# Cross-attention on one core: matmul operands of 1, 4 and 52 rows filled up to 128, and a 103-column transpose

## The reference

```python
text_p  = einsum('bld,dh->blh', H_l, W_text) + b_text      # x: 4 x 2048 x 512
audio_p = einsum('bsd,dh->bsh', H_a, W_audio) + b_audio    # ctx: 4 x 77 x 384
Q = layer_norm(text_p, g1, beta1)
K = layer_norm(audio_p, g2, beta2)
V = audio_p
scores  = einsum('blh,bsh->bls', Q, K) / sqrt(512)
alpha   = softmax(scores)
H_hyper = einsum('bls,bsh->blh', alpha, V)
H_hyper = einsum('blh,hk->blk', H_hyper, W_out) + b_out
return layer_norm(H_hyper + H_l, g_out, beta_out)
```

## Time and profile before

| | us |
|---|---|
| median of 3 runs | 270.38 |
| lowest and highest run | 270.07, 270.52 |
| the profiled execution's span | 269.2 |
| PE busy | 253.6 (94%) |
| DVE busy | 234.1 (87%) |
| ACT busy | 207.2 (77%) |
| POOL busy | 207.4 (77%) |

### The profile page before, as it was taken

The page is one execution under the profiler, slowest core; times in us unless marked ns, Lnnn a source line. Parts: engine busy times, 40 slices in busy tenths (PEclk is TensorE's granted clock), DMA queues, the critical chain, the costliest instruction groups (busy, mean ns, idle before and its releaser), DMA issues.

```text
span 269.2 us, 5946 instructions
## 1 busy us (share of the span) xinstructions
PE 253.6 (94%) x1667; PEld 232.3 (86%) x1667; DVE 234.1 (87%) x719; ACT 207.2 (77%) x516; POOL 207.4 (77%) x232
## 2 busy tenths in 40 slices
PE   7799999999999999999999999999999999999750
PEld 6578878989999989999999999999999999999520
DVE  3867489978999998999999999999999999998594
ACT  3766348235788888989988898888889889999681
POOL 6057440011189999999999999999999999999985
PEclk9999999999999999999999999999999999999997
DMA  6926099532225553544555445444444455442217
GB/s 195 266 80 195 2 280 393 151 131 72 78 80 168 167 175 138 175 160 157 177 181 179 168 169 173 165 156 156 156 158 159 169 169 162 160 171 108 106 46 273
DMA packets 19456, 43.25 MB, mean 161 GB/s; under 512 B 2050, under 2 KB 2382, under 8 KB 19434
## 3 DMA queue, kind: packets, MB, share of 16 engines
q1 hardware_dynamic: 18810, 41.96, 46.6%
q10 hardware_dynamic: 624, 1.06, 1.4%
HBM read 21.19 MB, written 16.78 MB: 141 GB/s over the span
## 4 chain that ended last, share of the span: by engine, by line
PE 73%; POOL 11%; DVE 5%; DMA 5%; ACT 2%; issue 2%; SPq 1%; POOLq 0%; ACTq 0%; DVEq 0%
PE psY L1332 24%; PE psY L1343 11%; PE psT L1261 9%; PE psO L1355 9%; PE psY L1336 4%; DMA zs<-in_ctx_dram 3%; POOL zs L464 3%; POOL zs L458 3%; PE psE L1311 2%; PE psE L1312 2%; DMA xs<-in_x_dram 2%; PE psY L1153 2%; POOL rstd L470 2%; POOL zs L494 1%; POOL zs L498 1%
## 5 line engine op out<-in xcount | busy, mean ns | idle before, releaser
L1332 PE MATMUL psY<-proj,x_hi 128*128 128x336 f32 x512 | 103.1, 323 | 0.0
L1332 PEld LDWEIGHTS psY<-proj,x_hi 128*128 128x128 f32 x512 | 82.7, 189 | 5.6 <-issue 0.4
L464 POOL TENSOR_TENSOR zs<-zs,shift 128x512 f32<-128x512 f32 x54 | 68.6, 1292 | 0.0
L458 POOL TENSOR_TENSOR zs<-zs,gain 128x512 f32<-128x512 f32 x54 | 68.5, 1290 | 0.0
L470 POOL TENSOR_TENSOR rstd<-stat_eps,neg_half 128x4 f32<-128x4 f32 x30 | 30.5, 1017 | 37.8 <-DVE stat_eps L970 35.9
L1343 PE MATMUL psY<-proj,x_lo 128*128 128x336 f32 (+1 forms) x256 | 50.7, 320 | 0.0
L958 DVE CUSTOM_DVE_ANT_0 waste_dve<-psY,xs,sums 128x515 bf16<-128x515 f32 x64 | 48.4, 756 | 2.3
L662 ACT ACTIVATE zs<-hid,shift,rstd 128x512 f32<-128x512 f32 x59 | 47.9, 812 | 0.0
L978 DVE SCALAR_TENSOR_TENSOR hid<-psO,inv_sum,xs 128x512 f32<-128x512 f32 x60 | 44.8, 746 | 2.0 <-PE psO L1355 0.8
L620 ACT ACTIVATE x_hi<-psT 128x512 fp32r<-128x512 f32 x64 | 38.1, 595 | 9.0 <-PE psT L1261 6.9
L856 DVE TENSOR_TENSOR x_lo<-psT,x_hi 128x512 fp32r<-128x512 f32 x64 | 43.6, 681 | 0.6 <-ACT x_hi L620 0.6
(11 more groups left out here) (264 smaller groups left out, 420.2 us busy)
## 6 DMA issues: line engine op xcount, KB each, us to landing
xs<-in_x_dram SPq DMA_DIRECT2D x64, 256.0 KB, 2.9
out_dram<-zs SPq DMA_DIRECT2D x29, 512.0 KB, 2.9
proj<-proj SPq DMA_DIRECT2D x4, 768.0 KB, 9.4
out_dram<-zs SPq DMA_DIRECT2D x6, 256.0 KB, 2.1
xs<-in_L_xattn_W_text_dram SPq DMA_DIRECT2D x4, 256.0 KB, 4.2
xs<-in_L_xattn_W_out_dram SPq DMA_DIRECT2D x2, 512.0 KB, 4.2
wa<-in_L_xattn_W_audio_dram SPq DMA_DIRECT2D x1, 768.0 KB, 6.7
zs<-in_ctx_dram SPq DMA_DIRECT2D x1, 462.0 KB
```

The source lines that it names most:

```text
L458: nc.gpsimd.tensor_tensor(zs[:, q, t, :], zs[:, q, t, :], gain[:], ALU.mult).then_inc(zg_ready, 1)
L464: nc.gpsimd.tensor_tensor(zs[:, q, t, :], zs[:, q, t, :], shift[:], ALU.add).then_inc(out_ready, 1)
L1332: nc.tensor.matmul(psY[:, t, to:to + HALF], x_hi[:, par, t, k * P:(k + 1) * P], proj[:, q, k, right * HALF:(right + 1) * HALF], start=(k = ...
```

## The change

Operands with fewer than 128 rows get 128. The tiles `cd_rows`, `pick` and `root_rows` have 128 partitions, and POOL fills them with zeros ahead of the writes to rows 0 to 3 or row 0. `kSqSum` gets 76 more columns, filled with zeros, so that line 1246 reads 128 columns in each block. The diagonals get all 128 rows in the last block as well (`krstd` has 128 rows already). A semaphore `zeros_ready` is raised four times by POOL and waited for by ACT, DVE and PE. The second transpose of `transpose_prob` and of the last step takes 103 columns in place of 128. `keep_busy` writes to another quarter of its bank.

```diff
-        cd_rows = sb("cd_rows", [4, 2, BS], F32R)
-        pick = sb("pick", [4, 2, P], F32R)
+        cd_rows = sb("cd_rows", [P, 2, BS], F32R)
+        pick = sb("pick", [P, 2, P], F32R)
...
-        kSqSum = borrow(0, BS)
+        kSqSum = borrow(0, len(KEYS) * P)
+        kSqLive, kSqPad = kSqSum[:, 0:BS], kSqSum[:, BS:len(KEYS) * P]
...
-        root_rows = x_hi[0:1, 0]
+        root_rows = x_hi[:, 0]
...
             nc.gpsimd.memset(mask[:], 1.0).then_inc(pool_own, 1)
+            nc.gpsimd.memset(kSqPad, 0.0).then_inc(zeros_ready, 1)
...
+            nc.gpsimd.memset(f32(root_rows), 0.0).then_inc(zeros_ready, 1)
+            nc.gpsimd.memset(f32(pick[:]), 0.0).then_inc(zeros_ready, 1)
+            nc.gpsimd.memset(f32(cd_rows[:]), 0.0).then_inc(zeros_ready, 1)
             pool.wait_ge(left_ready, 2)
...
+            act.wait_ge(zeros_ready, 4)
+            nc.scalar.activation(root_rows[0:1, 1, :], ROOT_BANK[0:1, :], ACT.Copy, scale=-1.0).then_inc(root_rows_ready, 1)
+            nc.scalar.activation(root_rows[0:1, 0, :], ROOT_BANK[0:1, :], ACT.Copy).then_inc(root_rows_ready, 1)
...
-                nc.vector.tensor_scalar(diag_hi[0:w, at:at + w], ident[0:w, 0:w], krstd[0:w, n:n + 1], None, ALU.mult).then_inc(diag_ready, 1)
+                nc.vector.tensor_scalar(diag_hi[:, at:at + w], ident[:, 0:w], krstd[:, n:n + 1], None, ALU.mult).then_inc(diag_ready, 1)
...
+            dve.wait_ge(zeros_ready, 4)
             for n in range(2):
-                nc.vector.tensor_tensor(pick[:, n, :], ident[0:4, n:n + 1].to_broadcast([4, P]),
+                nc.vector.tensor_tensor(pick[0:4, n, :], ident[0:4, n:n + 1].to_broadcast([4, P]),
...
-                    nc.tensor.matmul(bank[:, 0:P], ident[:], ident[:], start=True, stop=True)
+                    nc.tensor.matmul(bank[:, 3 * P:4 * P], ident[:], ident[:], start=True, stop=True)
...
-                        last = nc.tensor.matmul(A_BANK[0][:, at:at + w], ones_r[0:w, :], d[0:w, at:at + w], start=(n == 0), stop=(n == 1))
+                        last = nc.tensor.matmul(A_BANK[0][:, at:at + w], ones_r, d[:, at:at + w], start=(n == 0), stop=(n == 1))
...
+            pe.wait_ge(zeros_ready, 1)
             for n, (at, w) in enumerate(KEYS):
-                last = nc.tensor.matmul(A_BANK[1][0:w, n:n + 1], kSqSum[:, at:at + w], mean_of[:, 0:1], start=True, stop=True)
+                last = nc.tensor.matmul(A_BANK[1][:, n:n + 1], kSqSum[:, at:at + P], mean_of[:, 0:1], start=True, stop=True)
...
-                    last = nc.tensor.transpose(psE[:, (2 * t + 1) * P:(2 * t + 2) * P], f32(parts[:, t, 0:P]), ident[:])
+                    last = nc.tensor.transpose(psE[0:S + S_B, (2 * t + 1) * P:(2 * t + 2) * P], f32(parts[:, t, 0:S + S_B]), ident[:])
```

More of the change, by code:

```diff
@@ L193, in cross_attention @@
         ident_ready, ones_ready, gain_ready = sem("ident_ready"), sem("ones_ready"), sem("gain_ready")
+        zeros_ready = sem("zeros_ready")
         cxT_psum, cxT_ready = sem("cxT_psum"), sem("cxT_ready")
@@ L576, in _ @@
             act.wait_ge(root_psum, 1)
-            nc.scalar.activation(root_rows[:, 1, :], ROOT_BANK[0:1, :], ACT.Copy, scale=-1.0).then_inc(root_rows_ready, 1)
-            nc.scalar.activation(root_rows[:, 0, :], ROOT_BANK[0:1, :], ACT.Copy).then_inc(root_rows_ready, 1)
+            act.wait_ge(zeros_ready, 4)
+            nc.scalar.activation(root_rows[0:1, 1, :], ROOT_BANK[0:1, :], ACT.Copy, scale=-1.0).then_inc(root_rows_ready, 1)
+            nc.scalar.activation(root_rows[0:1, 0, :], ROOT_BANK[0:1, :], ACT.Copy).then_inc(root_rows_ready, 1)
             out_hi(1)
@@ L642, in _ @@
             act.wait_ge(cd_rows_psum, 1)
-            nc.scalar.activation(cd_rows[:, 0, :], C_BANK[0:4, 0:BS], ACT.Copy).then_inc(cd_hi_ready, 1)
+            nc.scalar.activation(cd_rows[0:4, 0, :], C_BANK[0:4, 0:BS], ACT.Copy).then_inc(cd_hi_ready, 1)
             score_hi(3)
@@ L865, in _ @@
                     dve.wait_ge(ksqsum_ready, k - 1)
-                nc.vector.tensor_tensor(kSqSum, kSq0 if k == 1 else kSqSum, KSQ[k], ALU.add).then_inc(ksqsum_ready, 1)
+                nc.vector.tensor_tensor(kSqLive, kSq0 if k == 1 else kSqLive, KSQ[k], ALU.add).then_inc(ksqsum_ready, 1)
             link(nc.vector.memset(kvar[:], 1.0))
@@ L876, in _ @@
             for n, (at, w) in enumerate(KEYS):
-                nc.vector.tensor_scalar(diag_hi[0:w, at:at + w], ident[0:w, 0:w], krstd[0:w, n:n + 1], None, ALU.mult).then_inc(diag_ready, 1)
+                nc.vector.tensor_scalar(diag_hi[:, at:at + w], ident[:, 0:w], krstd[:, n:n + 1], None, ALU.mult).then_inc(diag_ready, 1)
             for n, (at, w) in enumerate(KEYS):
                 dve.wait_ge(diag_ready, n + 1)
-                nc.vector.scalar_tensor_tensor(diag_lo[0:w, at:at + w], ident[0:w, 0:w], krstd[0:w, n:n + 1],
-                                               f32(diag_hi[0:w, at:at + w]), ALU.mult, ALU.subtract).then_inc(diag_ready, 1)
+                nc.vector.scalar_tensor_tensor(diag_lo[:, at:at + w], ident[:, 0:w], krstd[:, n:n + 1],
+                                               f32(diag_hi[:, at:at + w]), ALU.mult, ALU.subtract).then_inc(diag_ready, 1)
             def value(n):
@@ L930, in _ @@
             dve.wait_ge(cd_hi_ready, 1)
-            nc.vector.tensor_tensor(cd_rows[:, 1, :], C_BANK[0:4, 0:BS], f32(cd_rows[:, 0, :]), ALU.subtract).then_inc(cd_rows_ready, 1)
+            nc.vector.tensor_tensor(cd_rows[0:4, 1, :], C_BANK[0:4, 0:BS], f32(cd_rows[0:4, 0, :]), ALU.subtract).then_inc(cd_rows_ready, 1)
             lo_part(0, 0, 1)
@@ L1400, in last_transposes @@
                 nc.tensor.transpose(psE[:, 2 * t * P:(2 * t + 1) * P], f32(parts[:, t, S_B:2 * S]), ident[:])
-                nc.tensor.transpose(psE[:, (2 * t + 1) * P:(2 * t + 2) * P], f32(parts[:, t, 0:P]), ident[:]).then_inc(probT_psum, 1)
+                nc.tensor.transpose(psE[0:S + S_B, (2 * t + 1) * P:(2 * t + 2) * P], f32(parts[:, t, 0:S + S_B]), ident[:]).then_inc(probT_psum, 1)
             mix(0, END, 0, 3)
```

## The result

The changed kernel takes 272.67 us (median of 4 runs, 272.59 to 272.74), against 270.45 for the kernel before in the same comparison (4 runs, 270.07 to 271.01). The ratio is 1.0085, with a 95% interval of 1.0053 to 1.0117: slower, by 2.2 us. I had forecast 269.2, a range of 268.2 to 270.2, and "faster" at 0.80. All three are wrong.

What follows compares the result with a forecast made beforehand. The prediction took TensorE (PE), 73% of the chain of waits, as the bound. Gains of 1.07 + 0 + 0.10 + 0.05 + 0 + 0 = 1.22 us took 270.38 to 269.2 us, range 268.2 to 270.2.

Steps and rivals of the forecast that it cites:

- POOL's fills and the new waits: Start of the kernel: 1.9 us of fills on idle POOL, slowing at most three DVE instructions; counted 0, at worst 0.6.
- The cover: PE's idle 1.26 us ahead of 10.46, waiting for the context load, hides DVE's delay; without it 0.6 us would stand.
- The one-row matmuls: Line 1183, four matmuls ahead of the loop: padding removes excess distances, 1.07 us gained, bounds 0 and 1.07.
- that rows don't matter: Rival: the excess comes from waits or operand changes, which stay; 270.4, with a partial effect 269.8; chance 0.17.
- The variance matmul: Line 1246, 128 stationary columns in place of 52: padding costs between 0 and 0.04 us, taken as 0.
- The key scales: Line 1237, where the last two of six matmuls have 52 rows: 0.10 us gained, bounds 0 and 0.19.
- More partitions, not more columns: DVE's widened diagonals take more partitions, not more columns; counted within the 0 for fills and waits.
- The constants: Two pairs of 4-row matmuls (line 1287 first): 0.05 us gained at the first, 0 at the second, bounds 0 and 0.38 each.
- The transposes: Loop lines 1312 and 1401, 103 columns loaded in place of 128: distance stays 0.11 us, gain 0, upper end 1.3.
- The rival of 275.4: A 103-column load between full ones breaks the overlap in the loop, 0.10 us each, 6.2 in all; chance 0.05.
- The shift passes through the loop: From line 903 on every step hangs on the one before, so the 1.22 us saved reaches the end.

Runs made afterwards that it cites:

- the narrow diagonals: Changed kernel with late fills, DVE's last diagonal back to 52 rows and POOL zero-filling the rows below: 269.61 us, ratio 0.9972 against the kernel before.
- one early fill: Changed kernel with the fills of pick and cd_rows moved behind the inverse root, root_rows' fill left in place: 270.52 us, ratio 0.9958 against the kernel before.
- eight busy matmuls: Eight keep_busy matmuls added behind the first weight block's text transposes: 269.52 us in the changed kernel, 269.96 us in the kernel before.

## Why the prediction was wrong, and where it was right

**The step that failed is "POOL's fills and the new waits", which I counted as 0, at worst 0.6.** It named the fills, their 1.9 us and their stretch rightly (5.52 to 7.27). Two readings in it were wrong, the first and the third here; the second held.

- *How long DVE is held.* I took 0.2 us per instruction, from 0.68 against 0.49, where DVE's line 788 met the end of the work on POOL. Measured: one instruction held for as long as the fills last, 1.95 us for 0.49. The rows that I had read show the same: the fills of line 403 end at 2.19 + 2.48 = 4.67 us and line 788 at 4.27 + 0.68 = 4.95, again 0.28 us later. The 0.2 us was what was left of a run of fills, and no price of a meeting.
- *What is behind it on PE.* The cover that I named, PE's idle 1.26 us ahead of the context's transposes, did hold for the delay itself: with the clock kept up, PE still waited 0.40 us for the load.
- *What the delay does to PE.* I priced idle time as time only. The gap of 1.77 us was followed by 6.8 us at 1.2 GHz. That costs 0.72 on the context's transposes and 1.32 on gram(0), beside their start 0.58 late (how much of this is the load's landing in this execution is open): 2.62 us. With the gap filled and the fills left in place it is gone, but for 0.09 us at gram(1). The clock in the profile before was full from 6.8 us on, and I took it for granted rather than asking how near to the edge it was.

The sum of the forecast with this one term put right: 1.22 gained less 2.62 gives 1.4 slower; the trace shows 1.7, and the other 0.3 is the key scales.

**The other terms:**

- *The one-row matmuls, 1.07 us.* Right: 1.04. The shift falls from 2.62 to 2.25 at the first two (0.37, forecast 0.39) and to 1.58 behind the other two (0.67, forecast 0.68). My own rival, that rows don't matter, falls: the kernel with the fills and the waits but one-row operands keeps the stretch of 39.07 us. That the array runs empty at a change of rows was my reading of it; the runs show the price and not the mechanism.
- *The variance matmul, 0.* The shift goes from 1.58 to 1.52 across it, 0.06 gained where I had a cost of 0 to 0.04 or nothing; too small to tell.
- *The key scales, 0.10 gained.* Wrong in sign: PE waits for DVE's diagonals, from 37.10 + 0.23 to 37.66, and the shift grows from 1.52 us (transposes `turn`) to 1.86. "More partitions, not more columns" was true of DVE's work and not of its turn against POOL. With the narrow diagonals the padding gives its full 1.29 us up to the loop (39.06 to 37.77), against my 1.22.
- *The constants, 0.05 and 0.* Right: the shift goes from 1.79 to 1.76 at the first pair, and the first project starts 0.16 us behind the end of line 911 before (49.62, 49.46) and 0.14 after (51.38, 51.24): it waits for DVE. But DVE is not on the chain all the way from line 903, as I wrote; the chain of waits goes through ACT and DVE, and is back on PE from 46.79. At the second PE gained about 0.3 (1.73 to 1.46) and had it taken by the next wait: 1.73 again at the transposes.
- *The transposes, 0.* Right: 0.11 apart, loop unchanged within what single traces tell. The rival of 275.4 (a short load breaks the overlap) falls with it, though its sign was the result's.
- *The shift passes through the loop.* Right within 0.1 us: +1.73 at its start, +1.63 at 240 us.

My only way to "slower" from the fills was "a cover that fails", part of 0.06. The cover held, and the time was lost by a path that I had not listed. That path is not the fills' alone: the low clock came without them in two traces, and with all three of them in place it stayed away once the gap was filled.

## What to carry to other kernels

An idle gap of PE early in a kernel is not free because some load covers it: ask what the granted clock does behind it, and where the wait can't be removed, fill the gap with matmuls that nobody reads. Before placing fills on an idle POOL, look at what DVE does in those same microseconds, since one DVE instruction can be held for all of them. Padding to 128 rows was worth 0.19 us for each of the first two one-row matmuls and 0.34 for each of the other two, but pays only if the zeros and the wider writes cost nothing on the engines that feed it.

## What the runs showed that I had not expected

- A DVE instruction over 512 columns, held by one fill on POOL, took 1.18 us, by three in a row 1.95, and each time ended 0.28 us after the last fill. The kernel before had the same 0.28 in its own rows.
- After 1.77 us without a matmul the clock fell to 1.2 GHz for 6.8 us. It also fell for 3.4 us after gaps of 0.49, 0.75 and 0.83 us with few matmuls between them, and for 6.8 us after gaps of 0.55 and 1.36; in the kernel before it stayed full in spite of 1.26 us, and with one early fill in spite of 0.83, 0.65 and 0.46. Which of these a given execution meets varies; eight busy matmuls brought a spread of 4 to 6 us down to about 2.
- A weight load of 103 columns has a longer record (174 ns) than one of 128 (142 ns), at the same distance of the matmuls.
- At the same clock, an earlier landing of the context load moved gram(1) by 1.7 us between two executions of the kernel before, and a low clock near the end cost about 1 us in two others.
- 76 more rows in two of six DVE instructions changed which of DVE and POOL is held, 0.5 us for one against 0.4 for the other.
